# A hybrid block (state-space scan, WKV attention, two FFNs) on one core: when ScalarE changes its function table, with new unit orders and banks

## What is computed

```python
# stage H: state-space layer (512 inner channels, 16 states, 4 taps, rank 64)
xs, z = split(norm(x) @ W_in.T);  xc = silu(conv4(xs) + conv_b)
dt, B, C = split(xc @ W_x.T);     dt = softplus(dt @ W_dt.T + b_dt)
h[t] = exp(dt*A) * h[t-1] + dt*B*xc;  y = (h*C).sum(states) + D*xc
x = x + (y * silu(z)) @ W_out.T
# stage F: x = x + (silu(n @ Wg.T) * (n @ Wu.T)) @ Wd.T,  n = norm(x), 768 hidden
# stage K/R: WKV attention with 1024 channels
e  = exp(clip(k - w*steps_left)); eu = exp(clip(U + k))
x = x + (sigmoid(r) * (cumsum(e*v) + eu*v) / (cumsum(e) + eu)) @ Wo.T + bo
# stage F again, with the same weights
```

## Time before, and its profile

| | us |
|---|---|
| median of 3 runs | 1805.29 (1803.18 to 1805.94) |
| the profiled execution | 1803.37 |
| its span in the trace | 1801.3 |
| busy: PE, DVE, ACT, POOL | 1484.8, 1523.5, 1273.7, 1274.4 |

### The profile page before, as it was taken

One profiled execution on the slowest core, in us unless ns is written; L12 is line 12 of the kernel. 1 busy time (PEld: TensorE's weight loads), 2 busy tenths in 40 slices (PEclk: granted clock), 3 DMA queues, 4 the chain that ended last, 5 costly groups with the idle time before them and its releaser, 6 DMA issues. The chain is left out here.

```text
span 1801.3 us, 19199 instructions
## 1 busy us (share of the span) xinstructions
PE 1484.8 (82%) x4800; PEld 724.1 (40%) x4800; DVE 1523.5 (85%) x2045; ACT 1273.7 (71%) x2039; POOL 1274.4 (71%) x970
## 2 busy tenths in 40 slices
PE   4254487769889988989798888989897987999987
PEld 1011233234434453435444353444442552545364
DVE  3298889999989999998999998999999999984651
ACT  3567588776787768886788777877688576764742
POOL 0597987888588876888578886888588796650430
PEclk9676698989989999989999998999899998999999
DMA  7633445334345234533435234633345342211210
GB/s 225 224 117 130 148 134 184 97 129 132 130 122 191 70 129 156 170 115 123 140 122 175 91 116 140 206 100 124 123 135 159 102 137 83 94 44 51 62 41 29
DMA packets 163519, 225.21 MB, mean 125 GB/s; under 512 B 13457, under 2 KB 104082, under 8 KB 163410
## 3 DMA queue, kind: packets, MB, share of 16 engines
q1 hardware_dynamic: 163410, 223.99, 38.5%
...
## 5 line engine op out<-in xcount | busy, mean ns | idle before, releaser
L908 POOL TENSOR_TENSOR bu<-rep,bc 128x512 f32<-128x512 f32 x512 | 649.0, 1295 | 111.9 <-PE ps_y L1400 109.9
L1224 DVE TENSOR_TENSOR_SCAN ps_d<-ps_d,bu 128x512 f32<-128x512 f32 x384 | 458.2, 1214 | 62.6 <-POOL bu L908 51.7
L1068 ACT ACTIVATE ps_d<-rep,scale_a 128x512 f32<-128x512 f32 x512 | 337.6, 682 | 150.0 <-DVE bu L1231 130.3
L951 ACT ACT_TABLE_LOAD x237 | 304.1, 1283 | 108.0 <-PE ps_r L1349 34.1
L1349 PE MATMUL ps_r<-xT,wgu 128*128 128x512 f32 x768 | 360.0, 614 | 20.7 <-ACT hf L1090 6.9
L1349 PE MATMUL ps_r<-mix,wkv 128*128 128x512 f32 x512 | 251.3, 630 | 39.4 <-ACT yr L1115 12.7
L1231 DVE TENSOR_TENSOR bu<-ps_d,bc 128x512 f32<-128x512 f32 x384 | 253.3, 676 | 1.1
L1400 PE MATMUL ps_y<-bu,sel 128*32 128x512 f32 x1024 | 152.7, 671 | 106.1 <-DVE bu L1231 82.7
L1349 PEld LDWEIGHTS ps_r<-xT,wgu 128*128 128x128 f32 x768 | 144.9, 195 | 229.5 <-issue 222.3
L913 POOL TENSOR_TENSOR bu<-bu,bc 128x512 f32<-128x512 f32 x128 | 166.9, 1305 | 73.4 <-DVE bu L1224 72.6
L925 POOL TENSOR_TENSOR kv<-sums,kv 128x1024 f32<-128x1024 f32 x64 | 150.5, 2352 | 84.6 <-DVE sums L1310 66.8
...
## 6 DMA issues: line engine op xcount, KB each, us to landing
rep<-dd_scratch SPq DMA_DIRECT2D x128, 512.0 KB, 4.6
...
```

What stands on the lines that cost most here:

```text
L908: pool.tensor_tensor(bu[:, i % BU, :], rep[:, g % REP, 1, :], bc[:, 0, q, :], ALU.mult)\
L951: act.preload_act_table_set(name)
L1068: act.activation(ps_d[D_BANK[i]][:, :], rep[:, g % REP, 0, :], ACT.Exp, scale=scale_a[:, a, NQ * j + q:NQ * j + q + 1]).then_inc(decay_rea ...
L1224: dve.tensor_tensor_scan(states, d[:, :], bu[:, i % BU, :], 0.0, ALU.mult, ALU.add)\
```

## The change

1. `need` is called ahead of a unit's waits, and ahead of every unit it is called with the table that the next unit that needs one asks for. So a load is issued right behind the last unit of the other table, also ahead of units in between that need none. The semaphore increment that stood in front of each load is gone.
2. The five orders and the bank of each use are new. Units, their numbers and what they compute are the same. The new list "a" asks for 201 changes of table: 4 ahead of the first `a_decay`, 182 from there to the last one, 15 behind it. In 16 of the 201 places units that need no table stand between (27 units).

```diff
             def need(name):
                 if table[0] != name:
-                    act.sem_inc(carried.sem, 1)
                     act.preload_act_table_set(name)
                     table[0] = name
+            EXP_LN, SILU = "natural_log_exp_and_others", "silu_and_others"
+            TABLE_OF = {"ha_std": EXP_LN, "fa_std": EXP_LN, "ra_std": EXP_LN, "a_in": SILU, "a_xc": SILU, "a_dt": EXP_LN,
+                        "a_ln": EXP_LN, "a_decay": EXP_LN, "fa_gate": SILU, "ra_gate": SILU, "a_eu": EXP_LN, "a_e": EXP_LN,
+                        "a_recept": SILU, "a_rec": EXP_LN}
+            def upcoming(units, n):
+                for _, unit, _ in units[n + 1:]:
+                    if unit in TABLE_OF:
+                        return TABLE_OF[unit]
+                return table[0]
...
-                for t, unit, i in units:
+                for n, (t, unit, i) in enumerate(units):
                     m = s = f = r = t
+                    if n:
+                        need(upcoming(units, n - 1))
...
                     elif unit == "a_xc":
+                        need("silu_and_others")
                         act.wait_ge(conv_tap.sem, at(conv_tap, m, TAP_DONE[TAPS * i + TAPS - 1]))
-                        need("silu_and_others")
                         act.activation(xc[:, i, :], xc[:, i, :], ACT.Silu).then_inc(xc_ready.sem, 1)
```

The other units that need a table are changed as `a_xc` is. Of the lists, the beginnings and the ends that the prediction speaks of:

```diff
 "p", beginning
-        "hp_turn*2 p_in*4 p_xproj p_dt*4 p_in*4 p_y*2 hp_turn*2 p_in*3 p_y*2 p_in p_y p_in*2 p_y p_in p_y p_in p_y "
+        "hp_turn*2 p_in*5 p_xproj p_in*2 p_dt p_in p_dt*3 hp_turn*2 p_y*2 p_in*4 p_y*6 p_in*4 p_y p_xproj p_y "
 "p", end
-        "p_k p_v p_k p_v p_k p_y p_v p_post*2 p_k p_v fp_turn fp_turn2 fp_turn fp_turn2 fp_gate fp_up p_k p_v p_k "
-        "p_v p_wo p_wo2 p_k p_v fp_gate fp_up p_wo fp_gate fp_up fp_gate fp_up p_wo2 fp_gate fp_up fp_gate fp_up "
-        "p_wo fp_down fp_down2 fp_down fp_down2 fp_turn p_wo2 p_wo p_wo2 fp_turn2 fp_turn fp_turn2 rp_turn "
-        "rp_turn2 rp_turn p_k p_v p_recept rp_turn2 p_recept rp_gate*3 rp_up p_k p_v rp_up rp_gate p_recept p_k "
-        "rp_gate p_v rp_up p_recept p_k rp_gate p_v p_k p_v p_recept rp_up p_k p_v rp_up p_recept p_k p_v rp_up "
-        "p_recept rp_down rp_down2 rp_down rp_down2 p_k p_v p_recept p_wo p_wo2 p_wo p_wo2 p_wo p_wo2 p_wo p_wo2 "
-        "rp_turn rp_turn2 rp_turn rp_turn2 rp_gate*3 rp_up*3 rp_gate*3 rp_up*3 rp_down rp_down2 rp_down rp_down2"),
+        "rp_down rp_down2 p_k p_y p_v p_k p_v p_y p_k p_v p_post*2 p_k p_v p_k p_v fp_turn fp_turn2 fp_turn "
+        "fp_turn2 fp_gate fp_up fp_gate fp_up fp_gate fp_up fp_gate fp_up fp_gate fp_up fp_gate fp_up p_k p_v "
+        "fp_down p_k p_v p_wo p_wo2 fp_down2 fp_down p_wo p_wo2 fp_turn fp_down2 p_wo p_wo2 fp_turn2 fp_turn "
+        "fp_turn2 p_wo p_wo2 p_k p_v p_recept*8 rp_turn p_k p_v p_k rp_turn2 p_v rp_turn rp_turn2 rp_gate rp_up "
+        "rp_gate rp_up rp_gate rp_up rp_gate rp_up rp_gate rp_up rp_gate rp_up p_k p_v p_k p_v p_k p_v rp_down "
+        "rp_down2 p_k p_v rp_down rp_down2 p_k p_v p_wo p_wo2 p_wo p_wo2 p_wo p_wo2 p_wo p_wo2 rp_turn rp_turn2 "
+        "rp_turn rp_turn2 rp_gate rp_up rp_gate rp_up rp_gate rp_up rp_gate rp_up rp_gate rp_up rp_gate rp_up "
+        "rp_down rp_down2 rp_down rp_down2"),
 "a", beginning (first sequence)
- ha_std*2 ha_norm*2 ha_turn*2 a_tap*2 a_xc*2 a_tap*2 a_xc*2 a_xproj a_dt*2 a_in*2 a_ln*2 a_in*2 a_dt a_ln a_decay*7
+ ha_std*2 ha_norm*2 ha_turn*2 a_tap*2 a_xc*2 a_tap*2 a_xc*2 a_in a_xproj a_in*2 a_dt a_ln a_dt a_in a_ln a_dt a_ln
 "a", end, behind the last a_decay
- a_e a_eu a_recept a_e a_eu a_e a_eu a_rec fa_std fa_norm fa_std fa_norm a_e fa_turn*2 a_eu a_rec fa_gate a_rec ...
- ... a_rec ra_std ra_norm ra_std ra_norm ra_turn*2 ra_gate*6
+ a_e a_eu a_e a_eu a_e a_eu a_rec a_rec fa_std fa_norm a_e a_eu fa_std fa_norm a_e a_eu fa_turn*2 a_rec fa_gate ...
+ ... a_recept*8 ... a_rec*2 ra_std ra_norm ra_std ra_norm ra_turn*2 ra_gate*6
 "v", beginning
- hv_stats*2 hv_aggr*2 v_tap*6 v_scale v_tap*6 v_scan*2 v_hc v_scan v_hc ...
+ hv_stats*2 hv_aggr*2 v_tap v_scale v_tap*5 v_tap*6 hv_stats*2 hv_aggr*2 v_scan*2 v_hc ...
 "s", beginning
- s_xr s_wr*3 s_win*2 s_wo s_weights s_wkv*2 s_win s_wkv s_win s_x s_xc*2 fs_ffn s_win*2 s_xdbl fs_ffn*2 s_xc*2 s_win
+ s_win*2 s_xr s_wr*3 s_wo s_weights s_wkv*3 s_x s_win*2 fs_ffn s_win*2 s_xc*2 fs_ffn*2 s_xc*2 s_win s_sz s_xdbl s_win
```

More of the change, by code:

```diff
@@ new lines @@
+        "hp_turn*2 p_in*5 p_xproj p_in*2 p_dt p_in p_dt*3 hp_turn*2 p_y*2 p_in*4 p_y*6 p_in*4 p_y p_xproj p_y "
+        "p_dt*4 p_y*2 hp_turn*2 p_y*4 p_post p_y p_post p_y fp_turn fp_turn2 fp_turn fp_turn2 p_y fp_gate fp_up "
+        "p_y fp_gate fp_up fp_gate fp_up p_y fp_gate fp_up p_y fp_gate fp_up fp_gate p_y fp_up fp_down fp_down2 "
+        "p_y fp_down p_in*2 p_y fp_turn fp_down2 p_in*3 fp_turn2 p_y fp_turn fp_turn2 p_in*2 p_xproj p_in p_dt p_k "
+        "p_recept p_y p_recept*3 p_y p_recept*3 p_v p_recept p_dt p_k p_v p_y p_k p_v p_dt*2 p_y p_k p_v p_k p_v "
@@ new lines @@
+        "p_y p_k p_v p_y p_wo p_wo2 p_post p_y p_post p_wo p_y fp_turn p_k p_wo2 fp_turn2 fp_turn fp_turn2 p_y p_v "
+        "fp_gate fp_up fp_gate fp_up fp_gate fp_up fp_gate fp_up fp_gate p_y fp_up fp_gate fp_up p_k fp_down p_y "
+        "p_v fp_down2 fp_down fp_down2 p_y hp_turn*2 p_in*3 fp_turn fp_turn2 fp_turn fp_turn2 p_y p_in*2 p_wo p_in "
+        "p_wo2 p_in*2 p_wo p_wo2 p_y p_xproj rp_turn p_k p_v p_dt rp_turn2 rp_turn rp_turn2 p_recept rp_gate p_y "
+        "rp_up rp_gate rp_up rp_gate p_y rp_up rp_gate rp_up p_y rp_gate rp_up rp_gate rp_up p_y p_dt rp_down "
@@ new lines @@
+        "rp_down2 rp_down p_y rp_down2 p_k p_v p_y p_recept*2 p_k p_v p_recept p_k p_v p_recept p_y p_recept*2 p_k "
+        "p_v p_recept p_k p_v p_dt p_y p_k p_post*2 p_v p_wo fp_turn p_wo2 fp_turn2 p_y fp_turn fp_turn2 fp_gate "
+        "fp_up fp_gate fp_up p_y p_wo p_wo2 fp_gate fp_up fp_gate fp_up p_y fp_gate fp_up fp_gate fp_up p_y p_k "
+        "fp_down p_v p_dt p_y fp_down2 fp_down fp_down2 hp_turn*2 fp_turn p_wo p_wo2 fp_turn2 p_y fp_turn fp_turn2 "
+        "p_wo p_wo2 p_in rp_turn p_in p_k p_y rp_turn2 rp_turn rp_turn2 p_in*3 p_v p_in*2 p_y p_in p_xproj "
@@ new lines @@
+        "fp_turn p_wo2 p_y p_wo fp_turn2 fp_turn fp_turn2 p_wo2 p_in rp_turn p_in p_y p_in rp_turn2 rp_turn "
+        "rp_turn2 p_in*2 p_y p_in*2 p_xproj p_in p_dt p_y p_k p_v p_y p_recept p_k p_v p_recept*2 rp_gate rp_up "
+        "p_k p_v p_y rp_gate rp_up p_recept rp_gate rp_up p_y p_k p_v p_recept rp_gate p_y rp_up p_dt rp_gate "
+        "rp_up rp_gate p_y rp_up p_recept rp_down rp_down2 p_y rp_down rp_down2 p_post p_y p_post p_y p_recept p_k "
+        "p_v p_y p_recept p_k p_v fp_turn fp_turn2 fp_turn fp_turn2 p_wo p_wo2 fp_gate p_y fp_up fp_gate fp_up "
@@ new lines @@
+        "fp_gate fp_up p_k p_v fp_gate fp_up p_y p_wo p_wo2 fp_gate fp_up fp_gate p_y fp_up p_k fp_down p_v "
+        "fp_down2 fp_down p_y fp_down2 p_dt fp_turn p_dt hp_turn p_wo p_wo2 p_y fp_turn2 fp_turn fp_turn2 p_wo "
+        "p_wo2 hp_turn rp_turn p_in*2 p_k rp_turn2 rp_turn rp_turn2 p_in*2 p_v p_in*2 p_xproj p_y p_in*2 p_dt p_y "
+        "p_dt p_recept p_y p_k p_v p_recept p_y p_dt p_recept rp_gate rp_up p_k p_v rp_gate rp_up p_y p_recept "
+        "rp_gate rp_up p_k p_v p_recept rp_gate p_y rp_up rp_gate rp_up rp_gate rp_up p_y p_recept*2 rp_down "
@@ new lines @@
+        "rp_down2 rp_down rp_down2 p_y p_k p_v p_post*2 p_y p_recept p_k p_v p_dt p_wo p_wo2 fp_turn fp_turn2 "
+        "fp_turn fp_turn2 p_k p_y p_v fp_gate fp_up fp_gate fp_up fp_gate p_y fp_up fp_gate fp_up fp_gate fp_up "
+        "p_y fp_gate fp_up p_wo fp_down p_y p_wo2 p_k p_v fp_down2 p_y fp_down fp_down2 hp_turn*2 p_in*2 p_y "
+        "fp_turn p_in fp_turn2 fp_turn fp_turn2 p_in*2 p_wo p_wo2 p_in*2 p_wo p_wo2 p_xproj rp_turn p_y p_in p_k "
+        "p_v rp_turn2 rp_turn rp_turn2 p_dt p_recept p_y p_dt p_k p_v p_y p_recept*2 rp_gate rp_up p_k p_y p_v "
@@ L1054, in run @@
                     elif unit == "a_decay":
+                        need("natural_log_exp_and_others")
                         j, q, a = tile_of(i)
```

465 lines of the change are left out of this document (234 added, 231 removed), and 118 rows, old and new, of tables (BANKS, ORDER).

## The result

The changed kernel took 1759.9 us (median of four runs, 1756.5 to 1768.9) against 1805.6 (four runs, 1803.2 to 1807.0): ratio 0.9756, 95% interval 0.9716 to 0.9796. It is 46 us faster, where 17 were forecast.

A forecast was written before the change was run, and what follows sets the result against it. DVE was taken to bound the scans, latencies the head and PE the part behind. 1803.4 - 4 (head) - 9 (loads) + 0 (reordering) - 4 (behind the scans) = 1786.4, with the median 1.9 higher: 1788 us, range 1763 to 1808.

The forecast's parts named there:

- What bounds the kernel: Head: a chain of latencies; scans: DVE, 93% busy with 105.3 us of gaps; behind them PE until the last `p_wo`.
- the chain's share: Scans: loads' share of the chain that ended last, 5.6%, extended to 1489 us gives 61 us of loads.
- The loads in waits: Scans: fewer loads and loads in ACT's waits cut exposed load time from 262 to 186 us, worth 9 us.
- I price the rest of the reordering at 0: Scans: the new lists' other reordering gains or costs nothing, bounds -12 and +12 us.
- the lists give more: Rival: new orders also close gaps unrelated to loads, 25 us in the scans, 1767 us in all; chance 0.18.
- Loads ahead of units that need none: 16 places, 27 units: each may come 1.28 us later; 1.3 us lost at the end, 18 if all others counted.
- Head: Before the first scan: it starts near 75 us instead of 79.2, -4 us, bounds -7 and +1.
- Behind the scans: After the last `p_y`: -7 for gaps, +1.8 for one more `p_k`, +1.3 at the end: -4, bounds -12 and +6.
- Nothing changes: Rival: loads sit in gaps that something else ends, and the head's gain is given back; 1805 us, chance 0.12.
- Five tiles last: Rival, behind the scans: DVE's backlog on five last attention tiles outruns 3 us of slack, tail grows 11 us; chance 0.17.
- Drain: Rival: a table switch costs twice what the rows show, so the scans gain 18 us, 1779 us; chance 0.02.
- What I named as signs: Profile after: 201 loads with almost no idle ahead, first scan near 75 us, DVE 93.5% busy, last `p_y` near 1555.

The follow-up runs named there:

- the table: Old and new lists, each with loads behind waits, early with passes, early without, or none: 1806, 1781, 1773, 1756 us old; 1791, 1760 to 1766, 1753, 1741 new.
- with passes: Early loads also issued ahead of units that need none; on the kernel before's old lists 1780.7 us, against 1773.4 us with none ahead of such units.
- the second run: The changed kernel measured again, unchanged, against the kernel before on the same chip: 1766.1 us, ratio 0.9779.
- with the reload out of the way: Changed kernel without loads ahead of units needing none, plus a free buffer for the last sequence's second half of output weights: 1748.9 us, ratio 0.9681.

## Why the prediction was right and wrong

**What bounds the kernel.** Right. DVE's busy time in the scans stayed at 1381 to 1385 us in the kernels of the table, and the time followed its gaps. The whole of the loads cost 35.2 us there (1489.0 to 1453.8 without them); the chain's share had put them at 61 and my half of it, 30.5, is near.

**The loads in waits: the step that failed.** I wrote "Exposed load time goes from 262 us to 233 - 47 = 186, 29% less", and took 29% of the halved chain share, 9 us. That treats a microsecond of load as equally costly wherever it stands. Of it 11% was for fewer loads, which the table puts near nothing (50 us for 237, 48 to 50 for 201), and 18% for the idle time filled. The early loads alone, in the old lists, took 15.8 us out of the scans with passes and 18.9 without, which is 45% and 54% of what loads cost there. In the new lists it was more, 16 to 23 us with passes and 32 without (1478.5 to 1462.3, 1459.1 and 1455.7, and to 1446.8). So a load behind a wait is the costlier kind: 18.9 us for 69.8 of idle filled is 0.27 each, 35.2 us for 261.7 of loads 0.13 each. A reason would be that ACT has no backlog where it waits, so that its next result is due at once; no run tests that. The kernels with one table's loads early add that it matters which wait the load stood behind. The row that would have told me more was there: I took DVE's waits for ACT from their two largest entries, 25.9 us, and the sum of all is 43.8, of which 15.3 was the wait for `a_rec`.

**"I price the rest of the reordering at 0": the second step that failed.** The lists took 10.5 us out of the scans with the loads behind waits, 12.1 without loads, and 11 to 23 with early loads, near or beyond the bound of 12. The rival "the lists give more" named the right ground (gaps that have nothing to do with loads) and a size of 25 for loads and lists together; the profiled scans gave 26.7. Its time, 1767, was nearest to the 1760 to 1766 measured. What spoke against it, PE at 84%, was no obstacle: PE had gaps of 239 us in the scans before, and DVE's waits for its projections fell all the same.

**Loads ahead of units that need none.** Right in kind, and too small in the forecast: I had +1.3 at the end and named 18 us as the most. All of them cost 7 us in the old lists and 7 to 13 in the new ones. At the end it was as read: PE waits 4.29 us ahead of the last transposes with the pass, and 3.02 without.

**Head.** -4 forecast, -3.5 in the profile after, -2.9 in the second run. The first scan came at 75.67 (75 forecast). The number holds partly by luck. `p_xproj` took 3.74 us instead of 5.6 and the first `g_dt` started at 52.99, 2 us sooner than forecast. Then ACT's fourth `a_in` waited 2.86 us for the store of `sz`, with a load on either side of it, and the second `g_dt` came only at 62.80. The forecast had no such wait.

**Behind the scans.** -4 forecast, -4.0 measured (-3.6 in the second run). The terms: the new orders with loads behind waits need 164.6 + 68.5 = 233.1 us, the same as before, so the lists alone gave nothing; without passes it is 225.8, so -7.3 for the loads, and the passes give 3 to 4 of that back. I had -7 for the gaps, +1.8 for the `p_k` and +1.3 for the pass. So the sum is right by luck: what the loads and lists gave was 2 us more than I had, and the passes cost 2 us more.

**The rivals that fell.** "Nothing changes" fell with the result. "Five tiles last" did not turn the sign, but its slack was smaller than my 3 us: with the reload out of the way PE waits 2.83 us for the last tile, so the reload covered it by only 1.2. "Drain": `918.75` plus 1.28 is 920.03, and the next activation starts at 920.05; and 251 more loads cost 1.17 us each. The 1.38 us on top of each load that the Trainium skill gives (page "ScalarE: Activation LUTs", section "What ACT_TABLE_LOAD costs") is not seen in this kernel.

**What I named as signs.** 201 loads (202 with the first of all) with almost no idle ahead, DVE busy 94.5% in the scans (93.5 forecast), the last `p_y` at 1538.0 where 1555 was forecast. Of the 26.7 us in the scans the halves give 15.8 (early loads) and 10.5 (lists), together 26.3. That close an agreement is chance: in the changed kernel's second run the scans were 33.3 us shorter, not 26.7.
